# Four chained attention layers on one core: the scans' outer product from GpSimd to VectorE, token-shift mixes taken from the PSUM banks, the square on ScalarE, two narrow products in column groups, and another order of stages

## The reference

```
x = L0: cross attention to [ctx, x] (16 heads), + residual, RMS norm, MLP (gelu), + residual
x = L1: xa = LN(x); sx = shift(xa) - xa           # first token: state[1] - xa
        xxx = tanh((xa + sx*maa_x) @ maa_w1)      # 5 x 32 columns, then maa_w2
        x_j = xa + sx*(stack_j + xxx_j)           # j = k, w, v, r, g
        w = exp(-exp(td + tanh(x_w @ td_w1) @ td_w2)); r, k, v, g from products
        per step: a = k outer v; out = r.(u*a + s); s = a + w*s      # 64 steps
        x1 = x + (groupnorm(out)*g) @ Wo
        xc = LN(x1); sx2 = shift(xc) - xc         # first token: state[0] - xc
        x = x1 + sigmoid((xc+sx2*fmr) @ Wfr) * (relu((xc+sx2*fmk) @ Wfk)^2 @ Wfv)
x = L2: softmax attention to ctx, one head, + alpha * result
x = L3: attention to ctx, 32 query and 8 key heads, + residual, layer norm
```

## Time and profile before

| | |
|---|---|
| median of 3 runs | 1704.38 us (1703.74 to 1704.4) |
| the profiled execution | 1702.48 us, of which its span is 1700.6 us |
| PE busy | 1519.7 us, 89% |
| DVE busy | 1094.9 us, 64% |
| POOL busy | 680.9 us, 40% |
| ACT busy | 635.3 us, 37% |
| iterations with all three parts | 14, of about 98.6 us |

### The profile page before, as it was taken

One profiled execution on the slowest core, in us unless ns is written; L12 is line 12 of the kernel. 1 busy time (PEld: TensorE's weight loads), 2 busy tenths in 40 slices (PEclk: granted clock), 3 DMA queues, 4 the chain that ended last, 5 costly groups with the idle time before them and its releaser, 6 DMA issues.

```text
span 1700.6 us, 48519 instructions
## 1 busy us (share of the span) xinstructions
PE 1519.7 (89%) x21432; PEld 1139.8 (67%) x21432; DVE 1094.9 (64%) x1829; ACT 635.3 (37%) x1325; POOL 680.9 (40%) x620
## 2 busy tenths in 40 slices
PE   5877999999999999999998999999899999997765
PEld 4655777676777767677676767777676767765544
DVE  1347576767757676775767677575867767584732
ACT  2332433533443353434334344443434344342211
POOL 1044443535243353624335452533445253343510
PEclk9889999999999999999999999999999999998977
DMA  7021121304021130403113040311304040120300
GB/s 275 9 46 21 28 54 24 66 19 74 21 46 35 23 71 13 74 20 58 24 25 70 13 74 20 67 28 17 65 18 69 20 72 22 18 42 15 50 7 8
DMA packets 74257, 73.19 MB, mean 43 GB/s; under 512 B 28480, under 2 KB 63296, under 8 KB 73664
## 3 DMA queue, kind: packets, MB, share of 16 engines
q1 hardware_dynamic: 74048, 70.09, 20.9%
HBM read 32.32 MB, written 4.19 MB: 21 GB/s over the span
## 4 chain that ended last, share of the span: by engine, by line
PE 58%; DVE 23%; POOL 11%; issue 5%; ACT 2%; DMA 1%; DVEq 0%; POOLq 0%; SPq 0%; ACTq 0%
PE pw L395 21%; PE pw L373 8%; PE pw L595 7%; PE pw L379 5%; PE pw L589 5%; DVE mx L1068 5%; POOL ab L1027 4%; DVE ab L1211 4%; POOL ab L993 2%; DVE tB L1107 2%; PE pw L703 2%; PE pw L502 1%; DVE ptC L1258 1%; POOL c L1046 1%; DVE tC L1107 1%
## 5 line engine op out<-in xcount | busy, mean ns | idle before, releaser
L1211 DVE TENSOR_TENSOR_SCAN ab<-wS,ab 128x260 f32<-128x260 f32 x256 | 276.6, 1135 | 19.5 <-ACT ab L913 16.7
L1027 POOL TENSOR_TENSOR ab<-ab,kvrg 128x512 f32<-128x512 f32 x128 | 165.7, 1294 | 92.7 <-DVE ab L1211 92.7
L993 POOL TENSOR_TENSOR ab<-big,kvrg 128x512 f32<-128x512 f32 x128 | 184.9, 1449 | 6.0 <-DMA big<-kvrg 5.8
L1068 DVE TENSOR_REDUCE mx<-pw 128x16 f32<-128x1024 f32 (+1 forms) x128 | 149.3, 1205 | 27.5 <-PE pw L395 27.5
L1016 POOL TENSOR_TENSOR big<-big,xaB 128x512 f32<-128x512 f32 x80 | 95.4, 1207 | 171.6 <-DVE big L1190 171.6
L373 PE MATMUL pw<-big,wb 128*128 128x256 f32 x512 | 128.6, 395 | 0.5 <-issue 0.5
L589 PE MATMUL pw<-tA,wb 128*128 128x256 f32 x512 | 127.1, 398 | 0.7 <-DVE tA L1161 0.7
L595 PE MATMUL pw<-wb,ptA 128*128 128x256 f32 x512 | 119.4, 387 | 0.0
L978 POOL TENSOR_TENSOR vtmp_A<-mv_A,eps 128x2 f32<-128x2 f32 x16 | 3.1, 195 | 289.7 <-DVE mv_A L1088 289.7
L589 PEld LDWEIGHTS pw<-tA,wb 128*128 128x128 f32 x512 | 96.4, 195 | 28.6 <-issue 15.6
L373 PEld LDWEIGHTS pw<-big,wb 128*128 128x128 f32 x512 | 94.0, 193 | 24.4 <-issue 12.8
(11 more groups left out here) (212 smaller groups left out, 3210.7 us busy)
## 6 DMA issues: line engine op xcount, KB each, us to landing
big<-kvrg SPq DMA_DIRECT2D x256, 128.0 KB, 3.8
hT<-in_h SPq DMA_DIRECT2D x16, 512.0 KB, 5.7
wb<-in_wb SPq DMA_DIRECT2D x1, 5056.0 KB, 23.4
a<-in_x SPq DMA_DIRECT2D x16, 256.0 KB, 4.3
xB<-in_x SPq DMA_DIRECT2D x16, 256.0 KB, 2.9
m<-in_amask SPq DMA_DIRECT2D x64, 64.0 KB, 2.1
result<-c SPq DMA_DIRECT2D x16, 256.0 KB, 2.0
m<-in_mask SPq DMA_DIRECT2D x16, 128.0 KB, 2.6
```

Source lines behind the costliest of these rows:

```text
L993: G.tensor_tensor(ab[i % 4][:, :, :, 1:S + 1], vx[i % 3].rearrange("p j (b s) -> p j b s", b=NB), k, ALU.mult).then_inc(a_ok, 1)
L1027: G.tensor_tensor(ab[i % 4][:, :, :, 0:S], st[i % 2][:, :, :, 0:S], r, ALU.mult).then_inc(pd_ok, 1)
L1068: V.tensor_reduce(mx[:, 2 * j:2 * j + 2, g * p:g * p + g], pw[:, 2 * j:2 * j + 2, :].rearrange("p r (g s) -> p r g s", g=g), AXX, ALU.max) ...
L1211: last = V.tensor_tensor_scan(st[i % 2][:, j, :, :].rearrange("p b s -> p (b s)"), wS[:, i // 4, :, :].rearrange("p b s -> p (b s)"), ab[i ...
```

## The change

The outer product goes from GpSimd to DVE, in the same step as its scan. The mixes read the previous token from the PSUM bank, with the affine's weight folded into a per-channel factor (`aff[.., 2, ..]`); the first token of each sequence gets its own small addition from `first`, computed once. `xaC`, `sxC` and GpSimd's shift in part C are gone; `thC` is made like `tC`, in stage `cturn`. The square is an activation on ACT in stage `fk`. `mix1`'s product of 32 rows becomes four products of 64 tokens in four column groups, `pw1` two of 128 tokens in two. `ORDER` is another string.

```
-ORDER = "AABAACBABCCBACACCBBABCBAACBAACABBCBBBBBCCBBCABCBBCBABBCAACBBBBCABBBBCBBACCABACCCBB"
+ORDER = "AABACBABCBCCBBABCCBCBBCBBBACBBBABCBBACCBACAABCAACABBBACAABBCBBCABBBBBBCACCABCCABCB"
...
+            sp.dma_start(e0[:, :, :, :], e0_d).then_inc(ld_e, 16)          # at the start, once
...
 # PE, mix1
-                    for m in range(2):
-                        wide = P if m == 0 else 32
-                        for k in range(2):
-                            last = mm(kn((b4, b5)[m])[0:wide, m, :], w("m1", k)[:, m * P:m * P + wide], tB[:, k, :], start=(k == 0), stop=(k == 1))
-                        last.then_inc(m1_ps, 1)
+                    for k in range(2):
+                        last = mm(kn(b4)[:, 1, :], w("m1", k)[:, 0:P], tB[:, k, :], start=(k == 0), stop=(k == 1))
+                    last.then_inc(m1_ps, 1)
+                    for k in range(2):
+                        for b in range(NB):
+                            last = into(b5[group(b), 0:S], w("m1", k)[:, P:P + 32], tB[:, k, b * S:(b + 1) * S], k == 0, k == 1)
+                    last.then_inc(m1_ps, 1)
 # PE, pw1
-                        last = mm(kn(b5)[0:64, 0, :], w("td1", k), xm[1][:, k, :], start=(k == 0), stop=(k == 1))
+                        for c in range(TT):
+                            last = into(b5[64 * c:64 * c + 64, 0:P], w("td1", k), xm[1][:, k, tok(c)], k == 0, k == 1)
 # PE, fr: waits also until both banks of cturn are read
+                    pe.wait_ge(*read(SLOT["cturn", 0, t]))
+                    pe.wait_ge(*read(SLOT["cturn", 0, t] + 1))
 # ACT
+            def affine(to, m, src, name_b):
+                return A(to[:, 0, :], src, ACT.Identity, bias=vec(name_b, 0), scale=aff[:, m, 1, 0:1])
+            def fold_first():                                              # once, before the first norm0
+                act.wait_ge(ld_e, 16)
+                for m in range(3):
+                    for k in range(2):
+                        last = A(first[:, m, k, :], e0[:, (1, 0, 0)[m], k, :], ACT.Identity, bias=aff[:, m, 3, k:k + 1], scale=vec(("maax", "fmk", "fmr")[m], k))
+                last.then_inc(set_e, 1)
 # ACT, xturn: affine(tB) first, then xaB, then its first column
 # ACT, mix1 and pw1: four tanh of 32 x 64, two of 64 x 128 in place of one each
 # ACT, cturn
-                    A(xaC[:, :, :, 0:1], hT[t % 3][:, :, :, 0:1], ACT.Copy)
-                    shifted(xaC, tC, 1, kn(bank(k))[:, 0, :], "ln2w", "ln2b").then_inc(read(k)[0], 2)
+                    affine(tC, 1, kn(bank(k))[:, 0, :], "ln2b")
+                    affine(thC, 2, kn(bank(k))[:, 0, :], "ln2b").then_inc(ct_ok, 1)
 # ACT, fk
+                    act.wait_ge(*read(k))
+                    A(flat(kkS), flat(fkS), ACT.Square).then_inc(kk_ok, 1)
...
 # POOL: outer() and its calls, and the shift in cturn, are removed
...
 # DVE
+            def mixed(to, m, k, src):
+                v = seqs(to[:, k, :])[:, :, 1:S]
+                return V.scalar_tensor_tensor(v, seqs(src)[:, :, 0:S - 1], aff[:, m, 2, k:k + 1], v, ALU.mult, ALU.add)
+            def mixed_first(to, m, t):
+                v = to.rearrange("p k (b s) -> p k b s", b=NB)[:, :, :, 0]
+                return V.tensor_tensor(v, v, first[:, m, :, t * NB:(t + 1) * NB], ALU.add)
 # DVE, xturn
+                    affine(tB, 0, kn(b5)[:, 1, :], "ln1b").then_inc(xt_d, 1)
+                    V.tensor_scalar(xaB[:, 1, :, 1:S + 1], seqs(kn(b5)[:, 1, :]), vec("ln1w", 1), vec("ln1b", 1), ALU.mult, ALU.add).then_inc(xt_d, 1)
+                    dve.wait_ge(xt_d, t * 2 + 1)
+                    mixed(tB, 0, 1, kn(b5)[:, 1, :])
+                    dve.wait_ge(xt_sb, t * 2 + 1)
...
+                    mixed_first(tB, 0, t)
+                    mixed(tB, 0, 0, kn(b4)[:, 0, :]).then_inc(xin_ok, 1)
 # DVE, scan
+                    dve.wait_ge(vx_ok[i % 3], (t * (3, 3, 2)[i % 3] + i // 3 + 1) * 32)
                     if i >= 2:
                         dve.wait_ge(pd_ok, t * 8 + i - 1)
+                    if i >= 4:
+                        dve.wait_ge(rd_ps, t * 4 + i // 2 - 1)
+                    k = kS[:, i // 4, :].rearrange("p (b s) -> p b s", b=NB).unsqueeze(1).broadcast_to([P, 2, NB, S])
+                    V.tensor_tensor(ab[i % 4][:, :, :, 1:S + 1], vx[i % 3].rearrange("p j (b s) -> p j b s", b=NB), k, ALU.mult).then_inc(a_ok, 1)
 # DVE, cturn: two affines (tC, thC); mixed and mixed_first for tC (ff_d), then for thC (ff_d, read(k + 1), read(k))
 # DVE: L1258 (fk) and L1262 (l2k) are removed
```

More of the change, by code:

```diff
@@ L165, in build @@
         eps = sb("eps", [P, 4])
-        aff = sb("aff", [P, 2, 3, 2])
+        aff = sb("aff", [P, 3, 4, 2])
+        e0 = sb("e0", [P, 2, KT, B])
+        first = sb("first", [P, 3, KT, B])
         power = sb("power", [P, TT])
@@ L220, in build @@
         c3 = sb("c3", [P, TT, C])
-        fkS, kkS, gC, tS, uS, thC, sxC = (ptC[:, 512 * i:512 * (i + 1)].rearrange("p (k n) -> p k n", k=2) for i in range(7))
+        fkS, kkS, gC, tS, uS, thC = (ptC[:, 512 * i:512 * (i + 1)].rearrange("p (k n) -> p k n", k=2) for i in range(6))
         pbd, ptb = (ptC[:, 3584 + 128 * i:3712 + 128 * i].rearrange("p (t n) -> p t n", t=TT) for i in range(2))
@@ L825, in part_a @@
                     act.wait_ge(*full(k))
+                if t == 0 and name == "norm0":
+                    fold_first()
                 if name == "q0":
@@ L872, in part_b @@
                     act.wait_ge(xt_ps, t * 2 + 1)
-                    A(xaB[:, :, :, 0:1], hT[t % 3][:, :, :, 1:2], ACT.Copy)
-                    shifted(xaB, tB, 0, kn(b4)[:, 0, :], "ln1w", "ln1b").then_inc(xt_sb, 1)
+                    affine(tB, 0, kn(b4)[:, 0, :], "ln1b")
+                    A(xaB[:, 0, :, 1:S + 1], seqs(kn(b4)[:, 0, :]), ACT.Identity, bias=vec("ln1b", 0), scale=vec("ln1w", 0)).then_inc(xt_sb, 1)
+                    A(xaB[:, :, :, 0:1], hT[t % 3][:, :, :, 1:2], ACT.Copy).then_inc(xt_sb, 1)
                 elif name == "mix1":
                     act.wait_ge(m1_ps, t * 2 + 1)
-                    A(thB[:, 0, :], kn(b4)[:, 0, :], ACT.Tanh).then_inc(m1_sb, 1)
+                    A(thB[:, 0, :], kn(b4)[:, 1, :], ACT.Tanh).then_inc(m1_sb, 1)
                     act.wait_ge(m1_ps, t * 2 + 2)
-                    A(thB[0:32, 1, :], kn(b5)[0:32, 1, :], ACT.Tanh).then_inc(m1_sb, 1)
+                    for b in range(NB):
+                        last = A(thB[0:32, 1, b * S:(b + 1) * S], b5[32 * b:32 * b + 32, 0:S], ACT.Tanh)
+                    last.then_inc(m1_sb, 1)
                 elif name == "pv":
@@ L887, in part_b @@
                     act.wait_ge(pk_ps, t * 6 + 3)
-                    A(thB[0:64, 0, :], kn(b5)[0:64, 0, :], ACT.Tanh).then_inc(pk_sb, 1)
+                    for c in range(TT):
+                        last = A(thB[0:64, 0, c * P:(c + 1) * P], b5[64 * c:64 * c + 64, 0:P], ACT.Tanh)
+                    last.then_inc(pk_sb, 1)
                 elif name == "pr":
@@ L1030, in stage @@
                     inverse_root("B", t + 1, mv["B"][:, :, 1], 2)
[L1031 to L1035, removed]
                 elif name == "l2k":
@@ L1097, in seqs, with affine @@
                 return v.rearrange("p (b s) -> p b s", b=NB)
[L1099 to L1108 removed]
+            def affine(to, m, src, name_b):
+                return V.tensor_scalar(to[:, 1, :], src, aff[:, m, 1, 1:2], vec(name_b, 1), ALU.mult, ALU.add)
+            def mixed(to, m, k, src):
[4 more added lines that the diff above has]
+                return V.tensor_tensor(v, v, first[:, m, :, t * NB:(t + 1) * NB], ALU.add)
             def chain(t, k, ins):
@@ L1250, in part_c @@
                     dve.wait_ge(*full(k + 1))
-                    shifted(xaC, tC, 1, kn(bank(k + 1))[:, 1, :], "ln2w", "ln2b").then_inc(read(k + 1)[0], 2)
-                    dve.wait_ge(*read(k))
-                    dve.wait_ge(*read(k + 1))
-                    mixed(xaC, tC, "fmk").then_inc(ff_d, 1)
-                elif name == "fk":
-                    dve.wait_ge(sxC_ok, t + 1)
-                    for k in range(2):
-                        last = V.scalar_tensor_tensor(seqs(thC[:, k, :]), seqs(sxC[:, k, :]), vec("fmr", k), xaC[:, k, :, 1:S + 1], ALU.mult, ALU.add)
-                    last.then_inc(ff_d, 1)
-                elif name == "l2k":
-                    dve.wait_ge(*read(SLOT["fk", 0, t]))
-                    V.tensor_tensor(kkS, fkS, fkS, ALU.mult).then_inc(kk_ok, 1)
+                    affine(tC, 1, kn(bank(k + 1))[:, 1, :], "ln2b").then_inc(ct_d, 1)
+                    affine(thC, 2, kn(bank(k + 1))[:, 1, :], "ln2b").then_inc(ct_d, 1)
+                    dve.wait_ge(ct_d, t * 2 + 1)
+                    mixed(tC, 1, 1, kn(bank(k + 1))[:, 1, :])
+                    dve.wait_ge(ct_ok, t + 1)
+                    mixed_first(tC, 1, t)
+                    mixed(tC, 1, 0, kn(bank(k))[:, 0, :]).then_inc(ff_d, 1)
+                    dve.wait_ge(ct_d, t * 2 + 2)
```

(3 more changed lines are left out.)

56 lines of the change are left out of this document (19 added, 37 removed).

## The result

| | before | after |
|---|---|---|
| median, measured side by side | 1703.74 us (1700.34 to 1707.78, 7 runs) | 1692.11 us (1686.14 to 1695.68, 7 runs) |
| ratio | | 0.9934 [0.9912, 0.9956] |
| profiled span | 1700.6 us | 1690.3 us |
| mean granted clock | 0.972 | 0.962 |

A forecast was written before the change was run, and what follows sets the result against it. PE was taken to set the pace in full iterations. 1702.5 - 21 - 8 + 1 - 0.3 + 0.5 gave 1674.7 us for the profiled execution, 1.9 under the median: 1676.6, range 1662 to 1692.

The forecast's parts named there:

- A+B: Iteration with A and B alone: B's scans come before A's values, out0 and norm0 in the new order, -8 us.
- 14 full iterations: Iterations with A, B and C: -1.5 us each from shorter PE products and waits, -21 us in all.
- B+C: Iteration with B and C alone: scans are DVE's alone, with maxima between, +1 us (ends -2 and +4).
- C alone: Last stretch, only part C: cturn 0.3 us faster, fk waits for the thC mixes, -0.3 us in all.
- The narrow products: PE's mix1 and pw1 products in column groups: 0.28 and 0.5 us per tile, some 1.2 us less.
- exchange of turns: DVE instructions with two SBUF inputs and GpSimd's SBUF reads exclude each other for whole instructions; close scan steps take 2.95 us.
- the balance: DVE's work per tile, removed against added instructions: +1 to +5 us of 68, staying under PE.
- The walk: Stage-by-stage timing of PE, DVE, ACT and GpSimd in the new order, used to forecast PE's waits and the A+B iteration.
- that rival: DVE becomes the bound of the scan stretch through unlucky exchanges of turns: 1722 us (1706 to 1735), chance 0.15.
- The walked waits: PE's waits in a full iteration, stage by stage in the new order: sum 5.6 us against 6.1 before.
- the rival of better packing: PE near its 91.3 us with 3 us idle, 94.3 per full iteration: 1637 to 1655 us, chance 0.15.
- a rival of 0.05: PE's clock falls 0.02 in gaps at T 41 to 62, +1.8 us per full iteration: 1702 us, chance 0.05.

The follow-up runs named there:

- e3: The changed kernel with the two narrow products over 256 tokens in one column group again, as before the change: 1704.5 us, ratio 1.0008.
- e14: The changed kernel with the old ORDER and the two narrow products wide again: 1682.37 us, ratio 0.9877.
- e1: The changed kernel with the old ORDER string of the kernel before: 1678.8 us, ratio 0.9851.
- e9: The kernel before with the two narrow products in column groups (and their tanh in pieces) as the only change: 1708.36 us, ratio 1.0035.
- e5: The changed kernel with three more PE products per tile, results unused, ahead of the wait before up0: 1679.54 us, ratio 0.9862.
- e13: e7 with extra unused PE products at long waits in A alone, A+B and the last tile's part C: 1658.47 us, ratio 0.9741.
- e10: e5 with the old ORDER in the one iteration that has B and C alone: 1677.33 us, ratio 0.9842.
- e8: The changed kernel with the old ORDER and the outer product on GpSimd again: 1682.84 us, ratio 0.9884.
- e7: The changed kernel with the old ORDER in all iterations but the one with A and B alone, which has the new: 1677.63 us, ratio 0.9848.
- e11: The changed kernel with the old ORDER and one wait added: PE starts max11 only when DVE has done scan5: 1768.12 us, ratio 1.0385.

## Why the prediction came out as it did

By stretch, in us against before:

| | forecast | measured |
|---|---|---|
| start to A+B | +0.5 | +2.8 |
| A+B | -8 | -1.5 |
| 14 full iterations | -21 | -15.3 |
| B+C | +1 | +7.4 |
| C alone | -0.3 | -3.7 |
| sum | -27.8 | -10.3 |

**The narrow products.** Sized well, and the step held in this kernel. By form, after:

```profile
L398 PE MATMUL pw<-big,wb 128*64 128x128 f32 x128 | 10.5, 285 | 0.0
...
L398 PE MATMUL pw<-tB,wb 128*32 128x64 f32 x256 | 7.1, 231 | 0.0
```

Per tile 0.44 and 0.66 us where 0.28 and 0.5 were taken; against 1.11 and 1.08 before, 1.1 us saved for 1.2 forecast. "In a full iteration it comes off PE directly" is true of the changed kernel: e3 and after have the same waits of PE row by row, to 0.1 us over thirteen full iterations, and a full iteration at clock 1.00 falls from 97.6 us in mean (six in e3, one of them here below) to 96.3 (eight in after). The two falls that e3 has more are the smaller part of the 12.4 us.

```profile
647.56:745.18 97.62, 91.72 (x1340) 70.09 (x1339) 66.20 (x123) 40.61 (x83) 30.37 (x29) 1.00 0.25 41
```

But the step needs a condition that the prediction did not state, that no wait behind the saving takes it up. In the old order of the changed code about half is left: the waits for the maxima grew from 4.6 us in e14 to 13.2 in e1 over thirteen iterations. In the kernel before nothing is left (e9).

**DVE, GpSimd and the exchange of turns.** The mechanism held, the balance did not. In A+B after, DVE's scans of one step, the next step's outer product and its scans, and GpSimd's product beside them:

```profile
112.27 1.29 DVE L1231 TENSOR_TENSOR_SCAN ab<-wS,ab 128x260 f32<-128x260 f32 x2 [0.28 <-ACT ab L936]
113.47 0.67 DVE L1227 TENSOR_TENSOR ab<-big,kvrg 128x512 f32<-128x512 f32 x1
114.17 2.15 DVE L1231 TENSOR_TENSOR_SCAN ab<-wS,ab 128x260 f32<-128x260 f32 x2
113.64 1.54 POOL L1040 TENSOR_TENSOR ab<-ab,kvrg 128x512 f32<-128x512 f32 x1 [2.21 <-DVE ab L1231]
```

From the outer's start to the scans' end it is 2.85 us, forecast 2.95. The two scans behind GpSimd's product take 2.15 us, the two before it 1.29. (The prediction read 1.69 us of the earlier trace rows as a pair with GpSimd idle; GpSimd's outer products ran until 798.37 and reached into it.) That is the lock that I weighed with the Trainium skill's page "SBUF — State Buffer", section "Who interferes with whom". The clearest trace of it is the added first-token addition, in two places of the same code (count, shortest, median and longest in ns):

```profile
L1118 DVE TENSOR_TENSOR tB<-tB,first x16: 166/901/906, 80.6 to 1527.7; 128x8 f32<-128x8 f32 x16
L1118 DVE TENSOR_TENSOR tC<-tC,first x16: 157/163/168, 171.0 to 1621.3; 128x8 f32<-128x8 f32 x16
```

Eight elements per partition take 0.16 us, and 0.90 behind GpSimd's shift. The walk had put 0.7 of waiting there. DVE did not become the bound: that rival had 0.15, and the longest full iteration at clock 1.00 is 97.5 us, where it asked for 100. DVE's balance was put at +1 to +5 us of 68 per tile (its own terms give +0.5 to +3.9) and came out at -1.9, 68.1 to 66.2 in a full iteration: the scans wait less for a quieter GpSimd, and that was left out of the sum.

**The walked waits.** exp01 1.3 forecast and 1.3 measured, up0 1.2 and 1.3, zturn 0.85 and 0.85, k0 0.3 and 0.3; mix1 (0.55), sum0, sum3 and oturn1 (1.4 together) did not appear, and others of 0.3 to 0.5 did. In the iteration at 839.05 idle time is 5.3 us for 5.6, busy 90.5 for 91.3. At clock 1.00 a full iteration is 1.9 us shorter in mean than before, forecast 1.5. (In the rival of better packing 1704 - 60 - 9 is 1635, not 1637.)

**The clock.** This is the step that failed: the prediction priced PE's work at the full clock in all full iterations of the new order, and took the fall in the gaps as a rival of 0.05. The rival named the gaps (T 41 to 62), the level (0.02 of the clock) and nearly the price of an iteration (+1.8; by the means a fall costs 98.5 - 96.3 = 2.2 us), but had it in all fourteen, where it came in five. It got 0.05 because the iteration before stood waits up to 1.3 us at clock 1.00. What the new order has is three such waits within some 20 us, the last two ending 2.5 us apart, and then the clock falls in some iterations and not in others; why in these five stays open. They lose 2.2 us each, 11 us in all. Over the thirteen full steps e5 gives back 8.6 (its iterations at clock 1.00 are 0.2 longer, with the added products) and e1 10.3. The Trainium skill, page "TensorE: Matmul & The Clock Gate", section "HAM oscillation — how this bites in real kernels", describes the loss by single long gaps behind a DMA; in these full iterations no gap was over 1.3 us and the clock fell all the same, so the measurement decides.

**The ends.** A+B: -8 forecast, -1.5 measured. The walk was made with durations at full clock, while the rows had 0.88. In the runs without added products there the stretch took 83.0 to 85.7 us at clocks of 0.84 to 0.88 in the new order, and 86.3 to 89.9 at 0.83 to 0.88 in the old: at such clocks the order is worth some 3 us. e13 shows that the walk itself was right (77.5 us at clock 1.00, forecast 79) and that the clock ate it. B+C: +1 forecast, +7.4 measured, at a clock of 0.82 for 0.88; the old order there gives 3.6 us back (e10), and the changed code in the old order took 87.5 to 89.2 us at 0.82 to 0.83. The rest was not taken apart. C alone: -0.3 forecast, -3.7 measured, at a clock of 0.78 for 0.73. That need not be the change: e9 runs the same code as before there, in the same order, and took 76.6 us at 0.82 against 82.0 at 0.73. The start's +2.8 is within what the same code varies.

**Where the gain is.** Old order, outer product still on GpSimd, narrow products: 1682.8 (e8). Old order, outer on DVE, wide: 1682.4 (e14). Both changes: 1678.8 (e1). So 4 us each by the totals; by the full iterations 0.3 us each for the outer product (96.70 to 96.36) and 0.6 for the narrow ones. By the difference 12 to 17 us are left for the mixes from the banks and the square on ACT (an estimate from these runs, by the full iterations and by the totals, that takes the parts to add up). I had not priced them by themselves. They take GpSimd's shift in part C and DVE's six mixes with two SBUF inputs away, and end the wait for `thC` (1.0 in the earlier trace rows, no longer among e1's waits). That pair alone was not run, so its worth is not shown.

## What to carry to other kernels

Before booking a microsecond taken from the busiest engine, look whether a wait on another engine ends right behind it; if so it can be worth nothing (e9). When an order is changed, look at how close together the waits of PE lie, not only at their sum, and price each stretch at the clock that it will have. Where waits can't be closed, a few products that nobody reads, sized to the wait, cost little (0.2 us an iteration in e5) and can be worth more than the change itself: 12 us at one place here (after to e5), 19 us at the ends of the pipeline (e7 to e13).

## What the runs showed of the hardware

Three waits of 1.3, 0.85 and 1.3 us in some 20 us of otherwise dense work went with a fall of PE to 1.2 GHz in 5 of 14 identical iterations (one profiled execution), and in none of 28 when the last was filled (e5, e10). One wait of 5.1 us went with it in 14 of 14 (e11). With 5 to 6 us of idle time per iteration in other places, before and e1 stayed at 2.4 GHz in all full iterations. Where the pipeline is thin, the same code ran at different clocks: C alone 82.0 us at 0.73 (before) and 76.6 at 0.82 (e9). A record of 32 rows and 64 tokens in a column group cost 0.44/16 = 0.028 us in a run of sixteen, against 0.017 in the long runs of the earlier trace rows.
